# Layer 0 in one 512-column product for both halves of x, a PSUM bank per tile, and x's low half made by an adding transfer

## The reference

```python
base  = x[b] @ W.T                                   # layer 0, one weight for all batches
delta = (x[b] @ lora_A[label[b]]) @ lora_B.T * 0.5   # rank 32
x = x + base + delta
gi = sum(abs(x) <= thresholds)                       # layer 1: 8 ranges, one grid each
q  = clip(round(x / d[gi]) + zp[gi], 0, 63)
x = x + where(outside, 0, (q - zp[gi]) * d[gi])
x = x + x @ weight[adapter[b]].T                     # layer 2, a 1024x1024 weight per batch
x = x + (x @ B[adapter[b]].T) @ A[adapter[b]].T      # layer 3, rank 16
```

## Time and profile before

| What | Value |
|---|---|
| Time, median of 3 runs | 469.88 us (468.55 to 471.79) |
| Time of the profiled execution | 469.71 us |
| Its span, first to last instruction | 467.9 us |
| Mean granted TensorE clock | 0.995 |
| TensorE, VectorE, ScalarE busy | 456.6, 427.5, 316.4 us |

### The profile page before, as it was taken

One profiled execution on the slowest core, in us unless ns is written; L12 is line 12 of the kernel. 1 busy time (PEld: TensorE's weight loads), 2 busy tenths in 40 slices (PEclk: granted clock), 3 DMA queues, 4 the chain that ended last, 5 costly groups with the idle time before them and its releaser, 6 DMA issues.

```text
span 467.9 us, 7296 instructions
## 1 busy us (share of the span) xinstructions
PE 456.6 (98%) x3006; PEld 414.6 (89%) x3006; DVE 427.5 (91%) x406; ACT 316.4 (68%) x261; POOL 1.5 (0%) x11
## 2 busy tenths in 40 slices
PE   6999998999899999999999999999999999999996
PEld 6999998889898899989998899988998899988884
DVE  4788999999999998989799998899959999999983
ACT  5596969866597748947298563987349866665830
POOL 1000000000000000000000000000000000000000
PEclk9899999999999999999999999999999999999999
DMA  7982030236123534056322462142322432244242
GB/s 296 315 334 102 1 102 1 90 112 259 69 91 133 196 133 158 1 179 203 145 92 91 141 230 91 68 181 96 142 102 90 154 116 78 85 177 166 105 157 90
DMA packets 17077, 62.86 MB, mean 134 GB/s; under 512 B 2325, under 2 KB 3349, under 8 KB 12949
## 3 DMA queue, kind: packets, MB, share of 16 engines
q1 hardware_dynamic: 17044, 62.41, 37.2%
HBM read 54.01 MB, written 8.39 MB: 133 GB/s over the span
## 4 chain that ended last, share of the span: by engine, by line
PE 85%; DVE 8%; issue 3%; ACT 2%; DMA 1%; SPq 1%; DVEq 0%; ACTq 0%
PE l_ps L811 39%; PE l_ps L746 32%; PE l_ps L826 6%; DVE quant L607 3%; PE bx_ps L845 2%; DVE cand L581 2%; PE bx_ps L772 1%; PE l_ps L756 1%; DMA w_sb<-w 1%; PE l_ps L862 1%; DVE quant L601 1%; DVE x_lo L540 1%; PE bx_ps L779 1%; PE bx_ps L852 1%; ACT cand L415 1%
## 5 line engine op out<-in xcount | busy, mean ns | idle before, releaser
L811 PE MATMUL l_ps<-x,w_sb 128*128 128x256 f32 x896 | 197.0, 380 | 1.6 <-DVE x L661 1.2
L811 PEld LDWEIGHTS l_ps<-x,w_sb 128*128 128x128 f32 x896 | 169.2, 190 | 26.7 <-issue 4.2
L607 DVE COPY_PREDICATED quant<-mask,cand 128x2048 f32<-128x2048 int8 (+2 forms) x77 | 144.3, 1874 | 0.4
L425 ACT ACTIVATE mask<-magnitude,thr_bias 128x2048 fp8e5<-128x2048 f32 (+2 forms) x77 | 118.0, 1532 | 33.7 <-DVE quant L607 32.7
L415 ACT ACTIVATE cand<-x,inv_delta 128x2048 f32<-128x2048 f32 (+2 forms) x88 | 134.6, 1529 | 8.8 <-DVE quant L601 6.9
L581 DVE TENSOR_SCALAR cand<-cand,delta 128x2048 f32<-128x2048 f32 (+2 forms) x88 | 87.4, 993 | 10.6 <-ACT cand L415 10.3
L589 DVE TENSOR_SCALAR cand<-cand,lower,upper 128x2048 f32<-128x2048 f32 (+2 forms) x88 | 92.4, 1050 | 0.4
L746 PE MATMUL l_ps<-x_hi,w_hi 128*128 128x256 f32 x512 | 87.1, 292 | 3.5 <-DVE x_lo L540 1.9
L746 PE MATMUL l_ps<-x_hi,w_lo 128*128 128x256 f32 x512 | 83.0, 284 | 0.0
L746 PE MATMUL l_ps<-x_lo,w_hi 128*128 128x256 f32 x512 | 82.8, 284 | 0.0
L746 PEld LDWEIGHTS l_ps<-x_hi,w_hi 128*128 128x128 f32 x512 | 72.2, 193 | 8.6 <-issue 3.3
(11 more groups left out here) (62 smaller groups left out, 227.0 us busy)
## 6 DMA issues: line engine op xcount, KB each, us to landing
w_sb<-w SPq DMA_DIRECT2D x31, 1024.0 KB, 4.8
out<-x SPq DMA_DIRECT2D x32, 256.0 KB, 2.2
x_raw<-x SPq DMA_DIRECT2D x15, 512.0 KB, 6.2
a_raw<-a SPq DMA_DIRECT2D x8, 512.0 KB, 3.5
w_sb<-w SPq DMA_DIRECT2D x7, 512.0 KB, 7.6
b_sb<-b SPq DMA_DIRECT2D x8, 256.0 KB, 2.6
a_raw<-a SPq DMA_DIRECT2D x8, 128.0 KB, 6.3
x_raw<-w SPq DMA_DIRECT2D x1, 1024.0 KB, 6.7
```

The source lines that it names most:

```text
L425: act.activation(mask[:, m % MASKS, 0:n], magnitude[:, 0:n], ACT.Relu, bias=thr_bias[:, k:k + 1], scale=STEEP, saturate=False).then_inc(ma ...
L607: dve.copy_predicated(y, mask[:, m % MASKS, 0:n].bitcast(I8), t).then_inc(merged, 1)
L811: last = nc.tensor.matmul(l2_bank(b, q)[:, i * S:(i + 1) * S], w2_tile(b, o)[:, k * P:(k + 1) * P], x2[:, b % SLOTS, k * S:(k + 1) * S], s ...
```

## The change

From batch 3 on (`TWIN`) layer 0 multiplies `w0_hi` with both halves of x in one product of 512 columns, the high half to the low 256 columns of a bank, the low half to the high 256; the products with `w0_lo` and the closing one go to the low 256 columns. So a tile takes a whole bank and holds two sums. On drain ScalarE copies one sum of two tiles to `x2` (`copy_l0`) and VectorE adds the other from PSUM (`add_l0`), four times a batch, at candidates 5, 6 and twice at 7; TensorE waits for such an add at every second tile (`twin0`). From batch 2 on (`ADDED`) the low half of x is made without VectorE: ScalarE writes the negated high half (`negate_x`), and GpSimd issues a transfer that adds x to it (`add_x`). The next load of x waits for that. The split of batch 2 moves to the first unit. `AHEAD` gives steps 1 to 6 now 7, 6, 8, 8, 8 and 6 tiles (before 7, 8, 7, 7, 7 and 7), and the layer-3 work stands behind the second, third and sixth tile of a step (before the third, fourth and fifth). The tiles of these batches come in plain order.

```diff
-AHEAD = (21, 28, 36, 43, 50, 57, 64, 64)
+AHEAD = (21, 28, 34, 42, 50, 58, 64, 64)
+ADDED = 2
+TWIN = 3
...
-        x_hi = sb("x_hi", [P, 2, BW], F32R)
-        x_lo = sb("x_lo", [P, 2, BW], F32R)
+        x_split = sb("x_split", [P, 2, 2, BW], F32R)
...
-        l0_ps = ps("l0_ps", [P, 2, HW])
+        l0_ps = ps("l0_ps", [P, 4, CW])
...
-        def x0_halves(u):
+        def l0_parts(b, end):
+            return 2 * b + end // HALF if b < TWIN else 2 * TWIN + 4 * (b - TWIN) + end // 2
+        def x0_parts(u):
             b, first, n = UNITS[u]
-            return 2 * b + (first + n + HW - 1) // HW
+            return l0_parts(b, (first + n) // S)
+        def x0_tiles(b, p):
+            return x2[:, b % SLOTS, p * CW:(p + 1) * CW].rearrange("p (t s) -> p t s", t=2)
+        def l0_tile(b, o):
+            if b < TWIN:
+                return l0_ps[:, o // 2, o % 2 * S:(o % 2 + 1) * S]
+            return l0_ps[:, o % 4, 0:S]
+        def l0_pair(p, low):
+            return l0_ps[:, p % 2 * 2:p % 2 * 2 + 2, low * S:(low + 1) * S]
...
             def load_batch(b):
-                sp.wait_ge(x_split_done, x_pieces(b - 1, 1))
+                if b <= ADDED:
+                    sp.wait_ge(x_split_done, x_pieces(b - 1, 1))
+                else:
+                    sp.wait_ge(x_added, 16 * (b - ADDED))
                 sp.wait_ge(low_done, b)
                 load_x(b)
                 load_a0(b)
...
+            def add_x(b):
+                pool.wait_ge(x_neg_done, 2 * (b - ADDED + 1))
+                pool.dma_start(x_split[:, b % 2, 1, :], x_raw[:, :], accum_op=ALU.add).then_inc(x_added, 16)
+            for b in range(ADDED, B):
+                add_x(b)
...
+            def negate_x(b, h):
+                cols = slice(h * HW, (h + 1) * HW)
+                act.wait_ge(x_hi_done, x_pieces(b, h))
+                act.activation(x_split[:, b % 2, 1, cols], x_split[:, b % 2, 0, cols].bitcast(F32), ACT.Copy,
+                               scale=-1.0).then_inc(x_neg_done, 1)
             def split_batch(b):
                 split_x(b, 0)
                 split_x(b, 1)
+                if b >= ADDED:
+                    negate_x(b, 0)
+                    negate_x(b, 1)
...
             def drain_l0(b, h):
-                act.wait_ge(l0_done, 2 * b + h + 1)
+                act.wait_ge(l0_done, l0_parts(b, (h + 1) * HALF))
                 if b >= SLOTS:
                     act.wait_ge(x3_done, 4 * (b - SLOTS) + 4)
-                act.activation(x2[:, b % SLOTS, h * HW:(h + 1) * HW], l0_ps[:, h, :], ACT.Copy).then_inc(x0_done, 1)
+                act.activation(x2[:, b % SLOTS, h * HW:(h + 1) * HW], l0_ps[:, 2 * h:2 * h + 2, :].rearrange("p q s -> p (q s)"),
+                               ACT.Copy).then_inc(x0_done, 1)
+            def copy_l0(b, p):
+                act.wait_ge(l0_done, l0_parts(b, 2 * p + 2))
+                act.wait_ge(l2_done, 4 * (b - SLOTS) + 4)
+                act.wait_ge(x3_done, 4 * (b - SLOTS) + p + 1)
+                act.activation(x0_tiles(b, p), l0_pair(p, 1), ACT.Copy).then_inc(x0_copied, 1)
...
                         drain_low(1)
                     if j == 4:
                         low_rank_hi(1)
+                    if j == 6:
+                        split_batch(2)
                 elif u == 1:
                     if j == 1:
-                        split_batch(2)
                         drain_l0(1, 0)
                     if j == 4:
                         drain_l0(1, 1)
...
                             drain_low(s + 2)
                     if j == 4 and s + 2 < B:
                         low_rank_hi(s + 2)
+                    if s + 1 < TWIN:
+                        if j == 6:
+                            drain_l0(s + 1, 0)
+                    elif j in (5, 6):
+                        copy_l0(s + 1, j - 5)
                     if j == 7:
                         drain_bx(s - 1)
-                        drain_l0(s + 1, 0)
+                        if s + 1 >= TWIN:
+                            copy_l0(s + 1, 2)
                         split_bx(s - 1)
-                        if s + 1 < B - 1:
+                        if s + 1 < TWIN:
                             drain_l0(s + 1, 1)
+                        elif s + 1 < B - 1:
+                            copy_l0(s + 1, 3)
                 elif u == LAST:
+                    if j == 1:
+                        copy_l0(s, 3)
                     if j == 2:
                         split_a3(s - 1)
-                    if j == 3:
-                        drain_l0(s, 1)
...
+            def add_l0(b, p):
+                dve.wait_ge(x0_copied, l0_parts(b, 2 * p + 2) - 2 * TWIN)
+                dve.tensor_tensor(x0_tiles(b, p), l0_pair(p, 0), x0_tiles(b, p), ALU.add).then_inc(x0_done, 1)
...
                 s = UNITS[u][0]
                 if u == 0:
                     if j == 1:
-                        split_batch(1)
+                        split_x(1, 0)
+                        split_x(1, 1)
                     if j == 4:
                         low_rank_lo(1)
                 elif u == 1:
-                    if j == 1:
-                        split_batch(2)
                     if j == 5:
                         low_rank_lo(2)
                 elif s < B - 1:
                     if j == 1:
-                        if s + 2 < B:
-                            split_batch(s + 2)
                         drain_l2(s - 1, 0)
                     if j == 2:
                         drain_l2(s - 1, 1)
...
                             low_rank_lo(s + 2)
                     if j == 5:
                         drain_l2(s - 1, 3)
+                    if s + 1 >= TWIN:
+                        if j in (5, 6, 7):
+                            add_l0(s + 1, j - 5)
                     if j == 7:
                         split_bx(s - 1)
+                        if TWIN <= s + 1 < B - 1:
+                            add_l0(s + 1, 3)
                 elif u == LAST:
+                    if j == 1:
+                        add_l0(s, 3)
                     if j == 2:
...
-                if o == h * HALF and b > 0:
-                    pe.wait_ge(x0_done, 2 * (b - 1) + h + 1)
+                if o % HALF == 0 and b > 0:
+                    pe.wait_ge(x0_done, l0_parts(b - 1, o + HALF))
...
                     elif o == 0:
-                        pe.wait_ge(x_split_done, x_pieces(b, first // HALF))
-                    for w, v in ((w0_hi, x_hi), (w0_hi, x_lo), (w0_lo, x_hi)):
+                        pe.wait_ge(x_added, 16 * (b - ADDED + 1))
+                    for w, half in ((w0_hi, 0), (w0_hi, 1), (w0_lo, 0)):
...
-                            nc.tensor.matmul(dst, w[:, o, k * P:(k + 1) * P], v[:, b % 2, k * S:(k + 1) * S],
-                                             start=(o % 2 == 0 and v is x_hi and w is w0_hi and k == 0), stop=False)
+                            nc.tensor.matmul(dst, w[:, o, k * P:(k + 1) * P], x_split[:, b % 2, half, k * S:(k + 1) * S],
+                                             start=(o % 2 == 0 and w is w0_hi and half == 0 and k == 0), stop=False)
...
+            def twin0(b, o):
+                if o % 2 == 0:
+                    pe.wait_ge(x0_done, l0_parts(b, o - 2) if o >= HALF else l0_parts(b - 1, o + HALF + 2))
+                if o == 0:
+                    pe.wait_ge(x_added, 16 * (b - ADDED + 1))
+                for k in range(T):
+                    nc.tensor.matmul(l0_ps[:, o % 4, :], w0_hi[:, o, k * P:(k + 1) * P],
+                                     x_split[:, b % 2, :, k * S:(k + 1) * S], start=(k == 0), stop=False)
+                for k in range(T):
+                    nc.tensor.matmul(l0_tile(b, o), w0_lo[:, o, k * P:(k + 1) * P],
+                                     x_split[:, b % 2, 0, k * S:(k + 1) * S], start=False, stop=False)
...
                 last = nc.tensor.matmul(dst, b0_split[:, o * P:(o + 1) * P], low_split[:, b % 2, :], start=False,
-                                        stop=(o % 2 == 1))
-                if o in (HALF - 1, T - 1):
+                                        stop=(b >= TWIN or o % 2 == 1))
+                if o in (HALF - 1, T - 1) or b >= TWIN and o % 2 == 1:
                     last.then_inc(l0_done, 1)
...
+                if b >= TWIN:
+                    twin0(b, i)
+                    close0(b, i)
+                    return
...
-                if i == 0 and 0 < b < 3:
+                if i == 0 and b > 0:
                     low_rank0(b, 0)
                 main0(b, o)
-                if b > 2 or i >= HALF:
+                if i >= HALF:
                     close0(b, o)
...
                 for i, n in enumerate(range(AHEAD[s - 1], AHEAD[s])):
                     tile0(n)
-                    if i == 2:
+                    if i == 1:
                         for q in range(4):
                             low_rank3(s - 1, q)
-                    if i == 3:
+                    if i == 2:
```

(29 more changed lines are left out.)

13 lines of the change are left out of this document (4 added, 9 removed).

## The result

The changed kernel takes 481.12 us (480.1 to 481.48), against 469.94 for the kernel before on the same chip: a ratio of 1.024, 95% interval 1.021 to 1.027. So it is slower by 11 us; the forecast was 4.5 slower, with a range up to 480. A ratio can differ a little from that of the medians beside it. The profiled execution has a span of 479.5, 11.6 more than before.

The account below looks back on a forecast made before the run. TensorE was taken to set the pace, with VectorE having some 5 us of play a step; VectorE's last part starting 4.1 us later plus one add of 0.6 put 469.7 + 4.7 at 474.4 us, range 470 to 480.

Parts of the forecast that it names:

- the price of the twin product: TensorE's 512-column layer-0 product: 0.216 us each, from an f32 layer-2 product, so a tile takes 2.81 us, 0.19 less.
- the forecast's 2.3 us for each 0.010: From the weight-load rival: about 2.3 us go with each 0.010 us in the price of a twin product.
- the clock: TensorE at clock 1.00 (2.4 GHz) in the step used for prices; no term for a fall behind waits.
- The wait for the banks: Ahead of tile 4 of batch 3, TensorE waits 6.2 us for VectorE's add of tiles 0 and 1.
- the forecast's 402.4: Start of VectorE's first unit of the last batch, 399.6 + 0.4 + 2.4; before, it started at 398.30.
- Step 2: Ends at 187.3; its layer 3 is last, so the next layer 2 waits for three finishes, 1.5 us more: 188.8.
- steps 3 to 5: Each a layer 2 and eight tiles, 54.3 us, with 0.7 of waits in step 3: ending 243.8, 298.1, 352.4.
- Step 1: Begins with layer 2 of batch 0, at 80.0 in place of 80.68; reaches layer 3 at 128.6.
- The late place of layer 3: Layer 3 behind the sixth tile: VectorE's next unit waits for four finishes, starting at 131.4 against 131.0 before.
- Late transfer: Rival 1: batch 2's adding transfer takes longer than 11.4 us; at 15 us the end is 478.0; chance 0.18.
- The rival with no gain by width: Rival 2: a twin product takes 0.240 us and a tile 3.00, so the end is 480.6; chance 0.07.
- The rival in which the weight load paces the products: Rival 3: a twin costs 0.120 us like the others, a tile 2.04, end 459.6, not slower; chance 0.08.

Follow-up runs that it names:

- Holding the clock up: The changed kernel with 22 and 8 unread products of the identity run in TensorE's two waits: 477.2 us, 1.0175 to the kernel before.
- the best order found for the wide product: The changed kernel with layer 3 after the fifth tile, AHEAD from 21, 26, 34, and ScalarE's low-rank copy and split one candidate earlier in the last batch: 470.7 us, 1.0028.
- the replanned form: The changed kernel with layer 3 after the fifth tile and two tiles moved from step 1 to step 2: 472.87 us, 1.007 to the kernel before.

## Why the prediction was right in sign and wrong in size

**The steps that failed** are two. The first is the price of the twin product, "the nearest is an f32 product of layer 2 ... I take 0.216". It measured 0.230 in the kernel. What the forecast calls an f32 product is one of the two records of such a product, and it had the right width and the wrong type: a float32r product has some 0.013 us on top of its columns, which the forecast's own 0.120 for 256 columns already held (256 columns at 2.4 GHz are 0.107). Had I worked from that row the estimate would have been 0.213 + 0.013. By the forecast's 2.3 us for each 0.010, 0.014 is 3.2 us. Half the tile's saving went there, 0.09 a tile left of 0.19. The Trainium skill, TensorE: Matmul & The Clock Gate, Back-to-back issue gap, gives 216 ns isolated and 131 sustained for 512 columns; neither is met by float32r here, with 227 to 230 in a stream.

The second is the clock, a term put at nothing without a reason. The wait for the banks was forecast at 6.2 us and the products behind it at the price of the full clock, but TensorE comes out of such an idle stretch at 1.2 GHz: 2.3 us. A second stretch of it stands in the tail, behind a wait of 2.2 for ScalarE's copy that wasn't seen either: VectorE's last units begin 9.6 us later than before, and TensorE comes to that sum only 7.6 later, at 453.17 against 445.54:

```profile
445.54 0.59 PE L852 MATMUL bx_ps<-bx_parts,bx_sum 128*128 128x256 f32 x2
```

Holding the clock up gave back 3.5 us. With either of the two steps right, by these sums, the time would have been under 480.

**The sum.** VectorE's last units begin at 407.92, 5.5 past the forecast's 402.4: 3.2 of width and 2.3 of clock. (Step 2 ends at 191.68 against 188.8, and steps 3 to 5 add 2.8.) From there to the end are 71.6 us, against 70.2 forecast (472.6 of span less 402.4): 1.4, about what the slow products in the tail cost. 4.7 + 3.2 + 2.3 + 1.4 = 11.6, the measured difference of the spans.

**What held**, number by number. Step 1 starts at 80.09 (80.0). The add behind the wait starts at 167.25 (167.2), and TensorE waits 5.93 (6.2). The finishes are waited for at the end of step 2. Steps 3 to 5 are 56.05, 55.16 and 55.16, against 55.0, 54.3 and 54.3: about 0.9 longer, of which 8 tiles by 0.10 make 0.8. The late place of layer 3 was read rightly as what keeps VectorE from its next unit, and moving it back gained 6.1 us, more than any other single edit, though 1.5 of that is the clock in the tail.

**The rivals.** Late transfer was wrong: batch 2's transfer was issued at 53.31 and landed 7.5 us later, within the 11.4 that cost nothing.

```profile
53.31 1.00 POOL L358 DMA_DIRECT2D x_split<-x_raw  x1 [50.52 <-ACT x_split L392]
```
```profile
x_split<-x_raw POOLq DMA_DIRECT2D x1, 1024.0 KB, 7.5
```
```profile
x_split<-x_raw POOLq DMA_DIRECT2D x6, 1024.0 KB, 9.2
```

Of the last two lines the first is batch 2's transfer alone, the second the median of all six. VectorE was busy for 10.3 of the 12 us from 52 to 64. The rule on GpSimd's shut-out descriptors, in the Trainium skill, SBUF — State Buffer, SBUF: two separate sides, may be in the 9.2 us, and no run here takes it apart; it didn't decide. The rival with no gain by width would have been 480.6 by its own sum, near the measured time for another reason: the width does give 2.5 us. The rival in which the weight load paces the products has 0.12 for a twin and is out.

## What to carry to other kernels

Price a new form of product from rows of its own number type: take the columns from one row and the fixed part from another of that type, and only then ask for width. When a forecast has TensorE idle for several us, add the products behind the wait at half clock, or plan other work into it. Before a change that hands more buffers to an engine near its limit, write down the place of each hand-over in both queues: here moving layer 3 by one tile came with 6.1 us (1.5 of them by the clock) and the product's width with 2.5, and moving one copy by one candidate gained 1.6 where the best order found for the wide product gained nothing.

## What the runs showed of the hardware that I had not expected

A float32r product has a fixed 0.013 us beside its columns, from 256 to 512 columns, where plain float32 in two passes takes 0.216 for as many column times. Why is not settled. The granted clock fell to half behind idle stretches of 5.9, 3.6 and 8.1 us. Behind the 2.2 in the tail it fell in the profiled executions of the change, of the twin as two products and of the replanned form, and not in those of layer 3 moved and of the form without the transfer; behind the 1.6 to 2.3 at 11 us it fell in eight executions of twelve, so what waits of this length do isn't settled by the kernel. Behind 0.7, 1.1 and 1.4 it stayed. A fall cost 1.3 to 2.9 us. Adding transfers of 1 MB from SBUF to SBUF landed 7.2 to 13.8 us after their issue (medians of 7.8 to 9.7 in the kernels that have them) while all other engines ran, and the kernel that has them alone was not slower.
